# Pair interactions of a recommendation tower: products summed in groups of eight, larger rings, and fills placed between doubles

## The chip, the cores and the metric

The kernel runs on one core of a Trainium2 chip. The metric is the device time of one execution in microseconds, the median over several executions.

## The reference

For each of 2048 samples, 32 embedding rows of 64 numbers are gathered from 32 tables. `z` holds the sum of each row (32 values). For each of the 496 pairs i < j, `outer = x_i^T K_p x_j` with a 64 x 64 kernel of the pair's own. Then a small network follows, all in fp32:

```
z     = sum(x, axis=-1)                       # 32 values
outer = einsum('bpd,pde,bpe->bp', x_i, K, x_j)  # 496 values
h = concat([z, outer, dense_ctx])             # 544 values
h = relu(h @ W1 + b1)                         # 512
h = relu(h @ W2 + b2)                         # 256
y = h @ W3                                    # 1
```

## The kernel before, in words

The batch is worked off in four quarters of 512 samples (`NQ`, `QB`). A **stage** is a pair of features: 8 indirect DMAs from GpSimd (L176), each of 128 rows of one table, fill a slot of `gathered` (ring of `GR` = 4 stages, at most 4 gathers in flight). VectorE sums the rows (L287, `sum_x`), TensorE transposes the stage into `tr` (L328), and ScalarE copies it to `x_t` (L213, `keep_x`). There are 16 stages to a quarter, and `x_t` holds two quarters.

A **double** is a step of the pair work (`DOUBLES`, 128 to a quarter). TensorE multiplies two stages' halves with kernels of `k_sb` on 64 rows of the array each, side by side (L386 and L387, `multiply`), into one of `MR` = 3 slots of `m_ps`; each fp32 matmul shows as two passes. VectorE multiplies the result with `x_t` (L300, `product`) into `prod`, a ring of `PR` = 7. A slot of `m_ps` is free when its product is done: double p waits for product p - 3. TensorE then sums the products over partitions with 0/1 columns of `sel` into the bank `acc` (L398, `reduce`), for two doubles (a **quad**) with four matmuls side by side, and a product waits until the quad that read its slot of `prod` has been reduced. Doubles come in groups of `GROUP` = 4, and after the doubles of group g the two quads of group g - 1 are reduced. After 8 groups ScalarE copies `acc` to a block of `z_sb` (L247, `keep_z`); there are 4 blocks and a short one with the sums and `dense_ctx`.

All of `tr`'s users stand in one written order. `BEFORE` and `AFTER` give, by quarter and group, the **fills** ahead of a group's doubles or behind its reduction: transposed stages ("x"), the z sums ("s", L335), and the three layers of the quarter before ("h1" L339 and L341, "h2" L347, "y" L353). TensorE, ScalarE and VectorE walk the same order. In the first quarter stages are transposed close to their first use; stage a of a later quarter is transposed behind group 18 + 2a counted from the start of the quarter before, and its gathers are issued from three groups earlier on, each waiting for one more product (L170). The gathers of a stage also wait until the stage four places back is transposed and summed. The last quarter's layers run at the end (`layer1` into `m_ps`), after the last `keep_z`.

SyncE's queue loads indices, kernels (`k_sb`) and weights at the start, then per quarter the dense context and the store of `y`.

Of the kernel before, what the change touches and what calls it, by code (L numbers as in the profile page):

```python
# [6 lines left out]
DENSE, H1, H2 = 16, 512, 256  # L7
P = 128
NQ = 4
# [4 lines left out]
GR = 4  # L14
IN_FLIGHT = 4
PR = 7
# [19 lines left out]
GROUP = 4  # L36
# [3 lines left out]

GROUPS_OF_BLOCK = 8
NB = NG // GROUPS_OF_BLOCK
SUM_ROWS = F
ZLAST = SUM_ROWS + DENSE


def row_of(quad):
    return quad // (2 * GROUPS_OF_BLOCK), quad % (2 * GROUPS_OF_BLOCK)  # L50

# [4 lines left out]

BEFORE, AFTER = {}, {}


def group_of_stage(q, a):

    return 18 + 32 * (q - 1) + 2 * a


for _a in range(STAGES):
    _g = 0 if _a < 3 else min(FIRST[_a] // GROUP - (_a > 5), (4 * _a - 7) // 3)
    BEFORE.setdefault((0, _g), []).append(("x", 0, _a))
for _q in range(1, NQ):  # L70
    for _n in range(H1 // P):
        AFTER.setdefault((_q, 1 + 2 * _n), []).append(("h1", _q - 1, _n))
    for _n in range(H2 // P):
        AFTER.setdefault((_q, 9 + 2 * _n), []).append(("h2", _q - 1, _n))
    AFTER.setdefault((_q, 13), []).append(("y", _q - 1, 0))
    for _a in range(STAGES):
        AFTER.setdefault(divmod(group_of_stage(_q, _a), NG), []).append(("x", _q, _a))
    AFTER.setdefault((_q, 18), []).append(("s", _q, 0))
AFTER.setdefault((0, NG - 1), []).append(("s", 0, 0))
ORDER = [e for q in range(NQ) for g in range(NG) for e in BEFORE.get((q, g), []) + AFTER.get((q, g), [])]  # L80
PLACE = {e: n for n, e in enumerate(ORDER)}

def dlrm_tower(nc, ids, tables, kmat, dense_t, w1, b1, w2, b2, w3, out):
# [6 lines left out]
    with ctx:  # L90
# [13 lines left out]
        z_sb = sb("z_sb", [P, NB + 1, QB])  # L104
        z_nat = sb("z_nat", [P, 2, TILES, SUM_ROWS])
        w1_sb = sb("w1_sb", [P, NB + 1, H1])
# [48 lines left out]
        def _(pool):  # L155
# [5 lines left out]
            for G in range(NQ * STAGES):  # L161
# [4 lines left out]
                for n in range(GATHERS):  # L166
                    t, f = divmod(n, 2)
                    if q:

                        pool.wait_ge(prod_ready, GROUP * (group_of_stage(q, a) - 3) + n)  # L170
                    k = G * GATHERS + n
                    if k >= IN_FLIGHT:
# [4 lines left out]
                        out=gathered[:, G % GR, t, f, :], out_offset=None, in_=tables[2 * (STAGES - 1 - a) + f],  # L177
# [4 lines left out]
        def _(sp):  # L182
# [10 lines left out]
            for q in range(NQ):  # L193

                if q:
                    sp.wait_ge(tr_kept, place("h1", q - 1, H1 // P - 1))
                sp.dma_start(z_sb[SUM_ROWS:ZLAST, NB, :], dense_t[:, q * QB:(q + 1) * QB]).then_inc(dense_loaded, 16)
# [8 lines left out]
        def _(act):  # L206
            def keep_x(q, a):
                act.wait_ge(tr_filled, place("x", q, a))
                if q >= 2 and a == 0:

                    act.wait_ge(prod_ready, (q - 1) * ND)
                    act.wait_ge(reduced, (q - 1) * QUADS)
                nc.scalar.activation(x_t[:, q % 2, a, :], tr[:], ACT.Copy).then_inc(tr_kept, 1)  # L213
# [15 lines left out]
            def keep_sums(q):  # L229
                act.wait_ge(tr_filled, place("s", q, 0))  # L230
                nc.scalar.activation(z_sb[0:SUM_ROWS, NB, :], tr[0:SUM_ROWS, :], ACT.Copy).then_inc(tr_kept, 1)
# [13 lines left out]
            def keep_z(q, b):  # L245
                act.wait_ge(reduced, q * QUADS + 2 * GROUPS_OF_BLOCK * (b + 1))
# [3 lines left out]
            for q in range(NQ):  # L250
                for g in range(NG):
                    for what in BEFORE.get((q, g), ()):
                        keep(*what)
                    if g and g % GROUPS_OF_BLOCK == 0:
                        keep_z(q, g // GROUPS_OF_BLOCK - 1)
                    if g == 0 and q:
                        keep_z(q - 1, NB - 1)
                    for what in AFTER.get((q, g), ()):
                        keep(*what)
# [218 lines left out]
```

## Time and profile before

| what | us |
|---|---|
| median of 3 runs | 1012.58 (1011.55 to 1014.28) |
| the profiled execution | 1018.13 |
| its span in the profile | 1016.3 |
| TensorE busy, share of the span | 886.5, 87% |
| VectorE busy | 641.3, 63% |
| GpSimd busy | 483.6, 48% |
| ScalarE busy | 69.3, 7% |
| mean granted TensorE clock | 0.963 |
| product on VectorE, one | 1.219 (x512) |
| one gather on GpSimd | 0.943 (x512) |

Busy time of TensorE counts matmuls with modelled ends, so 87% is not 87% of its peak. The product's groups of instructions show 302.5 us of idle VectorE ahead of them, ended mostly by TensorE's matmuls of L387. The 40 slices of the span show TensorE at 9 tenths only from slice 9 on; ahead of that it is at 0 to 8 tenths and the granted clock falls to 5 tenths in places.

### The profile page before, as it was taken

How to read it: one execution, taken by the hardware profiler on the slowest of the kernel's cores; microseconds unless marked ns; L12 is line 12 of the kernel's file. 1: busy time of each engine (PE TensorE's matmuls, PEld its weight loads, DVE VectorE, ACT ScalarE, POOL GpSimd, SP SyncE). 2: the span in 40 equal slices, each digit the busy share in tenths (PEclk: the TensorE clock that was granted, in tenths of full speed). 3: DMA queues.
4: the chain of work that ended last, by engine and by line, in shares of the span. 5: the costliest groups of instructions: out<-in, count | busy, mean ns of one | idle time of the engine just before them, and what ended most of it. 6: DMA issues, size and time to landing. Idle time of an engine off the chain costs nothing.

```text
span 1016.3 us, 11896 instructions
## 1 busy us (share of the span) xinstructions
PE 886.5 (87%) x4608; PEld 311.6 (31%) x4608; DVE 641.3 (63%) x579; ACT 69.3 (7%) x113; POOL 483.6 (48%) x518
## 2 busy tenths in 40 slices
PE   0323579699999999998999999998999999999998
PEld 0111123223333333333333333323333333333333
DVE  0102257578887575687877656676787657688850
ACT  0000000000000001000000101000000101000001
POOL 5774735536565444555666444554556445400000
PEclk9956779999999999999999999999999999999999
DMA  9310101101111000110111010011101000000000
GB/s 348 107 27 15 27 14 19 21 12 23 23 21 23 17 17 18 20 21 20 22 23 22 15 19 17 19 22 19 21 19 24 15 17 19 19 1 1 1 1 0
DMA packets 19777, 28.20 MB, mean 28 GB/s; under 512 B 8901, under 2 KB 9413, under 8 KB 18825
## 3 DMA queue, kind: packets, MB, share of 16 engines
q0 software_dynamic: 16384, 16.81, 8.6%
q1 hardware_dynamic: 3336, 10.63, 2.9%
q8 instruction: 37, 0.61, 0.3%
q14 instruction: 20, 0.16, 0.1%
HBM read 27.40 MB, written 0.01 MB: 27 GB/s over the span
## 4 chain that ended last, share of the span: by engine, by line
PE 77%; another core or an unknown queue 8%; issue 7%; DVE 4%; DMA 2%; ACT 1%; SPq 1%; POOL 1%; DVEq 0%; POOLq 0%
PE m_ps L386 39%; PE acc L398 21%; PE tr L341 4%; DVE prod L300 3%; PE tr L328 3%; PE tr L347 2%; PE m_ps L387 2%; DMA w_sb<-in_w 2%; PE m_ps L341 1%; PE tr L339 1%; PE m_ps L347 1%; PE tr L353 1%; POOL gathered L176 1%; SPq L186 1%
## 5 line engine op out<-in xcount | busy, mean ns | idle before, releaser
L300 DVE TENSOR_TENSOR prod<-m_ps,x_t 128x1024 f32<-128x1024 f32 x512 | 604.3, 1219 | 302.5 <-PE m_ps L387 180.7
L176 POOL DMA_INDIRECT gathered<-in_tbl,idx x512 | 482.9, 943 | 403.4 <-DVE prod L300 178.2
L386 PE MATMUL m_ps<-x_t,k_sb 64*128 64x512 f32 x1024 | 501.4, 623 | 74.6 <-DVE prod L300 35.6
L387 PE MATMUL m_ps<-x_t,k_sb 64*128 64x512 f32 x1024 | 502.3, 624 | 0.0
L386 PEld LDWEIGHTS m_ps<-x_t,k_sb 64*128 64x128 f32 x1024 | 180.7, 191 | 346.9 <-issue 261.6
L398 PE MATMUL acc<-prod,sel 128*32 128x512 f32 x2048 | 247.0, 600 | 0.0
L387 PEld LDWEIGHTS m_ps<-x_t,k_sb 64*128 64x128 f32 x1024 | 180.6, 191 | 0.0
L398 PEld LDWEIGHTS acc<-prod,sel 128*32 128x32 f32 x2048 | 53.7, 109 | 176.5 <-issue 119.6
L328 PE MATMUL tr<-ident,gathered 128*128 128x128 f32 x256 | 44.5, 299 | 50.6 <-DMA gathered<-in_tbl,idx 41.4
L213 ACT ACTIVATE x_t<-tr 128x512 f32<-128x512 f32 x64 | 38.2, 597 | 471.7 <-PE tr L328 275.3
L287 DVE TENSOR_REDUCE z_nat<-gathered 128x8 f32<-128x512 f32 x64 | 43.1, 675 | 38.1 <-DMA gathered<-in_tbl,idx 38.1
L328 PEld LDWEIGHTS tr<-ident,gathered 128*128 128x128 f32 x256 | 28.5, 147 | 100.7 <-issue 87.4
L341 PE MATMUL tr<-z_sb,w_sb 128*128 128x512 f32 x96 | 44.4, 605 | 0.0
L341 PEld LDWEIGHTS tr<-z_sb,w_sb 128*128 128x128 f32 x96 | 17.2, 189 | 26.3 <-issue 26.3
L247 ACT ACTIVATE z_sb<-acc 128x512 f32<-128x512 f32 x16 | 9.6, 597 | 202.4 <-PE acc L398 129.5
L347 PE MATMUL tr<-h_sb,w_sb 128*128 128x512 f32 x48 | 22.2, 605 | 0.0
L217 ACT ACTIVATE h_sb<-tr,b_sb 128x512 f32<-128x512 f32 x12 | 8.2, 687 | 112.3 <-PE tr L341 112.3
L341 PE MATMUL m_ps<-z_sb,w_sb 128*128 128x512 f32 x32 | 14.8, 605 | 0.0
L339 PE MATMUL tr<-z_sb,w_sb 48*128 48x512 f32 x24 | 13.5, 641 | 0.0
L347 PEld LDWEIGHTS tr<-h_sb,w_sb 128*128 128x128 f32 x48 | 8.6, 189 | 13.6 <-issue 13.6
L341 PEld LDWEIGHTS m_ps<-z_sb,w_sb 128*128 128x128 f32 x32 | 5.8, 189 | 8.8 <-issue 8.8
L353 PE MATMUL tr<-h_sb,w_sb 128*1 128x512 f32 x16 | 7.5, 592 | 0.8 <-ACT h_sb L268 0.8
(24 smaller groups left out, 39.6 us busy)
## 6 DMA issues: line engine op xcount, KB each, us to landing
gathered<-in_tbl,idx POOLq DMA_INDIRECT x512
k_sb<-in_kmat SPq DMA_DIRECT2D x7, 1024.0 KB, 14.3
w_sb<-in_w SPq DMA_DIRECT2D x1, 1280.0 KB
k_sb<-in_kmat SPq DMA_DIRECT2D x2, 256.0 KB, 4.2
k_sb<-in_kmat SPq DMA_DIRECT2D x1, 512.0 KB, 6.4
w_sb<-in_w SPq DMA_DIRECT2D x1, 512.0 KB
idx<-in_ids SPq DMA_DIRECT2D x1, 256.0 KB, 2.7
z_sb<-in_dense_t SPq DMA_DIRECT2D x4, 32.0 KB
```

Of the source, the lines that this page charges most:

```text
L176: nc.gpsimd.indirect_dma_start(out=gathered[:, G % GR, t, f, :], out_offset=None, in_=tables[2 * (STAGES - 1 - a) + f], in_offset=bass.Ind ...
L213: nc.scalar.activation(x_t[:, q % 2, a, :], tr[:], ACT.Copy).then_inc(tr_kept, 1)
L287: nc.vector.tensor_reduce(z_nat[:, q % 2, :, 2 * a:2 * a + 2], gathered[:, G % GR, :, :, :], axis=AX.X, op=ALU.add).then_inc(x_summed, 1)
L300: nc.vector.tensor_tensor(prod[:, p % PR, :, :], m_ps[:, p % MR, :, :], other, ALU.mult).then_inc(prod_ready, 1)
L328: last = nc.tensor.transpose(tr[:, t * P:(t + 1) * P], gathered[:, G % GR, t, :, :].rearrange("p f d -> p (f d)"), ident[:])
L339: nc.tensor.matmul(to, w1_sb[0:ZLAST, NB, n * P:(n + 1) * P], z_sb[0:ZLAST, NB, :], start=True, stop=False)
L341: last = nc.tensor.matmul(to, w1_sb[:, b, n * P:(n + 1) * P], z_sb[:, b, :], start=False, stop=(b == NB - 1))
L347: last = nc.tensor.matmul(to, w2_sb[:, c, n * P:(n + 1) * P], h1_sb[:, c, :], start=(c == 0), stop=(c == H1 // P - 1))
L353: last = nc.tensor.matmul(to, w3_sb[:, c:c + 1], h2_sb[:, c, :], start=(c == 0), stop=(c == H2 // P - 1))
L386: nc.tensor.matmul(m_ps[:, p % MR, 0, :], k_sb[0:D, d, :], x_t[0:D, q % 2, a0, :], start=True, stop=True)
L387: nc.tensor.matmul(m_ps[:, p % MR, 1, :], k_sb[D:P, d, :], x_t[D:P, q % 2, a1, :], start=True, stop=True).then_inc(unit_done, 1)
L398: last = nc.tensor.matmul(acc[c * 32:c * 32 + 32, :], sel[:, 30 - 2 * row:62 - 2 * row], prod[:, (q * ND + 2 * n + c // 2) % PR, c % 2, :] ...
```

## The change

- `GROUP` is 8 and a quarter has 16 groups. A group's four quads are reduced in one go after the fifth double of the next group (`BEHIND` = 5). A block of `z_sb` is 4 such groups.
- `PR` is 12. `x_t` is one ring of `XR` = 20 stages in place of two quarters; `keep_x` waits until the last product that uses the old stage is done.
- `BEFORE`/`AFTER` become `AHEAD`, by single doubles: a fill stands ahead of a double. In the first quarter stage a comes three doubles ahead of its use, the last five earlier. In later quarters stage a comes at double 88 + 8a from the start of the quarter before, "h1" ahead of doubles 11, 19, 27, 35, "h2" 43 and 51, "y" 59, the z sums 84. Gathers are issued from 24 doubles ahead of their transpose.
- Layer one at the end is cut in two: short block and blocks 0 and 1 for all four outputs ahead of the wait for the last `keep_z`, blocks 2 and 3 behind it.
- `gathered` has the tiles outermost; `DENSE` has another spelling.

```diff
-PR = 7
+XR = 20
+PR = 12
-GROUP = 4
+GROUP = 8
+BEHIND = 5
...
+LAST_USE = [0] * STAGES
+for _d, _e in enumerate(DOUBLES):
+    for _a in _e:
+        LAST_USE[_a] = _d
-GROUPS_OF_BLOCK = 8
+GROUPS_OF_BLOCK = 4
...
-def group_of_stage(q, a):
-    return 18 + 32 * (q - 1) + 2 * a
+def step_of_stage(q, a):
+    return ND * (q - 1) + 88 + 8 * a
...
-    _g = 0 if _a < 3 else min(FIRST[_a] // GROUP - (_a > 5), (4 * _a - 7) // 3)
-    BEFORE.setdefault((0, _g), []).append(("x", 0, _a))
+    _s = FIRST[_a] - 3
+    AHEAD.setdefault((0, max(0, min(_s, 86 - 2 * (STAGES - 1 - _a))) if _a > 1 else 0), []).append(("x", 0, _a))
...
-        x_t = sb("x_t", [P, 2, STAGES, QB])
-        gathered = sb("gathered", [P, GR, TILES, 2, D])
+        x_t = sb("x_t", [P, XR, QB])
+        gathered = sb("gathered", [P, TILES, GR, 2 * D])
...
-                        pool.wait_ge(prod_ready, GROUP * (group_of_stage(q, a) - 3) + n)
+                        pool.wait_ge(prod_ready, step_of_stage(q, a) - 24 + n)
...
             for q in range(NQ):
-                for g in range(NG):
-                    for what in BEFORE.get((q, g), ()):
+                for d in range(ND):
+                    for what in AHEAD.get((q, d), ()):
                         fill(*what)
-                    for d in range(GROUP * g, GROUP * (g + 1)):
-                        multiply(q, d)
-                    if g:
-                        reduce(q, g - 1)
-                    elif q:
-                        reduce(q - 1, NG - 1)
-                    for what in AFTER.get((q, g), ()):
-                        fill(*what)
+                    multiply(q, d)
+                    if d % GROUP == BEHIND - 1:
+                        if d >= GROUP:
+                            reduce(q, d // GROUP - 1)
+                        elif q:
+                            reduce(q - 1, NG - 1)
             reduce(LAST, NG - 1)
             pe.wait_ge(dense_loaded, 16 * NQ)
+            pe.wait_ge(tr_kept, place("s", LAST, 0))
+            pe.wait_ge(z_kept, NQ * NB - 1)
+            pe.wait_ge(prod_ready, NQ * ND)
+            for n in range(H1 // P):
+                layer1_begin(n, m_ps[:, n // 2, n % 2, :])
             pe.wait_ge(z_kept, NQ * NB)
             for n in range(H1 // P):
-                layer1(n, m_ps[:, n // 2, n % 2, :], h1_summed)
+                layer1_end(n, m_ps[:, n // 2, n % 2, :], h1_summed)
```

## Rows read from the trace of the kernel before

**Rows 1.** The page: busy us (share of the span) and instructions of an engine.
```profile
PE 886.5 (87%) x4608; PEld 311.6 (31%) x4608; DVE 641.3 (63%) x579; ACT 69.3 (7%) x113; POOL 483.6 (48%) x518
```
**Rows 2.** Windows: stretch, length, busy us of each engine, granted clock, DMA share, GB/s.
```profile
41.70:146.58 104.88, 49.81 (x197) 17.77 (x196) 31.19 (x29) 3.58 (x6) 61.70 (x66) 0.69 0.11 21
146.58:320.20 173.62, 158.84 (x900) 54.24 (x896) 131.83 (x120) 10.49 (x18) 98.34 (x105) 0.98 0.11 21
320.20:544.85 224.65, 216.83 (x1154) 76.03 (x1152) 159.56 (x145) 17.71 (x29) 120.20 (x129) 1.00 0.10 20
544.85:772.50 227.65, 218.67 (x1156) 76.69 (x1152) 159.84 (x145) 16.87 (x28) 120.64 (x129) 0.99 0.10 19
772.50:980.30 207.80, 207.78 (x1112) 73.66 (x1108) 154.29 (x137) 12.86 (x21) 57.38 (x61) 1.00 0.06 11
```
**Rows 3.** Timeline of TensorE, gathers over: start us, us, line, operation, [idle before <-releaser].
```profile
947.40 1.93 PE L398 MATMUL acc<-prod,sel 128*32 128x512 f32 x16
949.25 0.69 PE L386 MATMUL m_ps<-x_t,k_sb 64*128 64x512 f32 x1
...
949.79 0.59 PE L386 MATMUL m_ps<-x_t,k_sb 64*128 64x512 f32 x1
...
952.36 0.59 PE L386 MATMUL m_ps<-x_t,k_sb 64*128 64x512 f32 x1
...
952.89 1.06 PE L398 MATMUL acc<-prod,sel 128*32 128x512 f32 x8
```
**Rows 4.** Timeline of ScalarE: copies of transposed stages, among gathers and after them.
```profile
303.01 0.60 ACT L213 ACTIVATE x_t<-tr 128x512 f32<-128x512 f32 x1 [11.53 <-PE tr L328]
315.20 0.60 ACT L213 ACTIVATE x_t<-tr 128x512 f32<-128x512 f32 x1 [11.60 <-PE tr L328]
...
887.86 0.60 ACT L213 ACTIVATE x_t<-tr 128x512 f32<-128x512 f32 x1 [5.49 <-PE tr L328]
...
899.42 0.60 ACT L213 ACTIVATE x_t<-tr 128x512 f32<-128x512 f32 x1
```
**Rows 5.** Timeline of VectorE, among gathers and after them.
```profile
290.57 0.68 DVE L287 TENSOR_REDUCE z_nat<-gathered 128x8 f32<-128x512 f32 x1
291.16 4.85 DVE L300 TENSOR_TENSOR prod<-m_ps,x_t 128x1024 f32<-128x1024 f32 x4
...
309.30 1.23 DVE L300 TENSOR_TENSOR prod<-m_ps,x_t 128x1024 f32<-128x1024 f32 x1 [1.18 <-PE m_ps L387]
...
950.43 3.49 DVE L300 TENSOR_TENSOR prod<-m_ps,x_t 128x1024 f32<-128x1024 f32 x3 [0.60 <-PE m_ps L387]
```
**Rows 6.** Timeline of TensorE among gathers, around that product.
```profile
308.08 0.59 PE L386 MATMUL m_ps<-x_t,k_sb 64*128 64x512 f32 x1
...
310.67 0.66 PE L386 MATMUL m_ps<-x_t,k_sb 64*128 64x512 f32 x1 [0.28 <-DVE prod L300]
```
**Rows 7.** Timeline of GpSimd and TensorE in the first quarter.
```profile
187.66 0.95 POOL L176 DMA_INDIRECT gathered<-in_tbl,idx  x1 [2.21 <-issue]
...
216.84 0.94 POOL L176 DMA_INDIRECT gathered<-in_tbl,idx  x1 [10.77 <-DVE z_nat L287]
...
203.90 1.19 PE L386 MATMUL m_ps<-x_t,k_sb 64*128 64x512 f32 x1 [6.45 <-issue]
```
**Rows 8.** Chain that ended last, in order of time: start us, us, what.
```profile
349.48 1.05 PE tr L339 x2
350.53 3.63 PE tr L341 x8
...
366.78 3.63 PE tr L341 x8
```
**Rows 9.** Waits of TensorE from 320.2 to 980: us in total, times, longest.
```profile
PE tr L328 <- ACT z_sb L231: 4.5, 2, 2.4
```
**Rows 10.** Timeline of TensorE at the end of the pair work.
```profile
984.78 1.09 PE L339 MATMUL m_ps<-z_sb,w_sb 48*128 48x512 f32 x2 [0.81 <-ACT z_sb L247]
```
**Rows 11.** Windows: the stretch behind the longest of those waits.
```profile
687.00:692.30 5.30, 4.10 (x14) 2.12 (x16) 1.00 (x1) 1.18 (x2) 0.68 (x1) 0.68 0.04 6
```

More of the change, by code:

```diff
@@ L76 @@
     for _a in range(STAGES):
[L77 to L80, printed above, removed]
+        AHEAD.setdefault(divmod(step_of_stage(_q, _a), ND), []).append(("x", _q, _a))
+    AHEAD.setdefault((_q, 84), []).append(("s", _q, 0))
+ORDER = [e for q in range(NQ) for s in range(ND) for e in AHEAD.get((q, s), [])]
@@ L81 @@
 PLACE = {e: n for n, e in enumerate(ORDER)}
+KEEP_Z = {GROUP * GROUPS_OF_BLOCK * b + BEHIND - 1: b - 1 for b in range(1, NB)}
+KEEP_LAST_Z = BEHIND - 1
 def dlrm_tower(nc, ids, tables, kmat, dense_t, w1, b1, w2, b2, w3, out):
@@ L208, in keep_x @@
                 act.wait_ge(tr_filled, place("x", q, a))
[L209 to L213, printed above, removed]
+                G = q * STAGES + a
+                if G >= XR:
+                    old_q, old_a = divmod(G - XR, STAGES)
+                    act.wait_ge(prod_ready, old_q * ND + LAST_USE[old_a] + 1)
+                nc.scalar.activation(x_t[:, G % XR, :], tr[:], ACT.Copy).then_inc(tr_kept, 1)
             def keep_h1(q, n):
@@ L250, in _ @@
             for q in range(NQ):
-                for g in range(NG):
-                    for what in BEFORE.get((q, g), ()):
+                for s in range(ND):
+                    for what in AHEAD.get((q, s), ()):
                         keep(*what)
-                    if g and g % GROUPS_OF_BLOCK == 0:
-                        keep_z(q, g // GROUPS_OF_BLOCK - 1)
-                    if g == 0 and q:
+                    if s in KEEP_Z:
+                        keep_z(q, KEEP_Z[s])
+                    if q and s == KEEP_LAST_Z:
                         keep_z(q - 1, NB - 1)
-                    for what in AFTER.get((q, g), ()):
-                        keep(*what)
             keep_z(LAST, NB - 1)
@@ L336, in sums, with layer1_begin, layer1_end @@
                 last.then_inc(tr_filled, 1)
-            def layer1(n, to, done):
-                nc.tensor.matmul(to, w1_sb[0:ZLAST, NB, n * P:(n + 1) * P], z_sb[0:ZLAST, NB, :], start=True, stop=False)
-                for b in range(NB):
+            def layer1_begin(n, to):
+                nc.tensor.matmul(to, w1_sb[0:ZLAST, ZSHORT, n * P:(n + 1) * P], z_sb[0:ZLAST, ZSHORT, :],
+                                 start=True, stop=False)
+                for b in range(NB - 2):
+                    nc.tensor.matmul(to, w1_sb[:, b, n * P:(n + 1) * P], z_sb[:, b, :], start=False, stop=False)
+            def layer1_end(n, to, done):
+                for b in (NB - 2, NB - 1):
                     last = nc.tensor.matmul(to, w1_sb[:, b, n * P:(n + 1) * P], z_sb[:, b, :],
@@ L385, in multiply @@
                     pe.wait_ge(prod_ready, p - MR + 1)
-                nc.tensor.matmul(m_ps[:, p % MR, 0, :], k_sb[0:D, d, :], x_t[0:D, q % 2, a0, :], start=True, stop=True)
-                nc.tensor.matmul(m_ps[:, p % MR, 1, :], k_sb[D:P, d, :], x_t[D:P, q % 2, a1, :],
+                nc.tensor.matmul(m_ps[:, p % MR, 0, :], k_sb[0:D, d, :], x_t[0:D, (q * STAGES + a0) % XR, :],
+                                 start=True, stop=True)
+                nc.tensor.matmul(m_ps[:, p % MR, 1, :], k_sb[D:P, d, :], x_t[D:P, (q * STAGES + a1) % XR, :],
                                  start=True, stop=True).then_inc(unit_done, 1)
@@ L393, in reduce @@
                     pe.wait_ge(z_kept, q * NB + g // GROUPS_OF_BLOCK)
-                for n in (2 * g, 2 * g + 1):
+                for n in range(GROUP // 2 * g, GROUP // 2 * (g + 1)):
                     _, row = row_of(n)
@@ L449 @@
                     continue
-                p = pair_index(min(i, j), max(i, j))
-                k_l[half * D:half * D + D, d, t * D:t * D + D] = k_in[p] if i < j else k_in[p].T
-                w1_l[b, 32 * ((d % 2) * 2 + half) + 2 * row + t] = w1_in[F + p]
+                k_l[half * D:half * D + D, d, t * D:t * D + D], w1_l[b, 32 * ((d % 2) * 2 + half) + 2 * row + t] = pair(i, j)
     for f in range(F):
-        w1_l[NB, F - 2 - 2 * (f // 2) + f % 2] = w1_in[f]
-    w1_l[NB, SUM_ROWS:ZLAST] = w1_in[w1_in.shape[0] - DENSE:]
+        w1_l[ZSHORT, F - 2 - 2 * (f // 2) + f % 2] = w1_in[f]
+    w1_l[ZSHORT, SUM_ROWS:ZLAST] = w1_in[w1_in.shape[0] - DENDE:]
     arrays = {
```

66 lines of the change are left out of this document (34 added, 32 removed).

## The prediction

> **What bounds the kernel now.** I read the busy shares first, then the stretches, then single instructions of each. TensorE is busy for 87% of the span [rows 1], but matmul ends are modelled, so the share says only where to look. By stretches [rows 2] the span falls into four parts: doubles 0 to 23 (104.9 us, TensorE busy for 49.8 and at a mean granted clock of 0.69), doubles 24 to 127 (173.6), quarters one and two (224.7 and 227.7), quarter three up to its last two reductions (207.8). The last part has almost no gathers and is TensorE at its pace: from one reduction to the next 952.89 - 947.40 = 5.49 us [rows 3], which is 12 passes (8 of the four doubles, 4 of the reduction, 0.429 each from 949.79 and 952.36) or 5.14, and 0.35 of switching.
>
> The stages with gathers are slower. With gathers over, two groups with one transposed stage take 899.42 - 887.86 = 11.56; with gathers on, 315.20 - 303.01 = 12.19 [rows 4]. A difference of 0.6 per eight doubles is not TensorE's work. The row that shows it is the first product after a reduction: in the tail its double's second pass begins 0.64 ahead of it (949.79, 950.43) [rows 3, 5], among gathers 1.22 ahead (308.08, 309.30) [rows 5, 6], and the fourth double of the group then waits until 310.67. VectorE's product chain is therefore just critical after each reduction, twice per eight doubles. The worst such delays come in long unbroken runs of gathers: 15 gathers from 187.66 with no pause (the next is at 216.84, after 10.77 idle), and in it TensorE stands for 6.45 us before 203.90 [rows 7]. I call such late completions slips; what makes them the trace does not say.
>
> **Part 1: eight doubles per reduction.** Removed: one of two switches per eight doubles, 0.35. Added: a reduction of 8 passes in one go, in which only three filled slots of m_ps stand ready for VectorE (MR stays 3; 12 product slots do not help, since a double needs an m_ps slot). Step by step, from t, the start of the second pass of the double ahead of a reduction:
> - reduction begins at t + 0.53 (952.36 to 952.89), takes 1.85 for four passes (947.40 to 949.25), so 1.85 + 4 x 0.43 = 3.57 for eight; the next double's second pass is 0.54 later: t + 4.64 [rows 3];
> - its product starts 0.64 later: t + 5.28. VectorE has long run dry, its three products took only 3.4;
> - the next double that a reduction follows needs the fifth product from here (slot free). Products follow each other by (3.48 - 1.22)/2 = 1.13 [rows 5]: the fifth starts at t + 9.80 and ends at t + 11.02;
> - TensorE's waiting double then has its second pass 0.65 after that end (309.30 + 1.23 = 310.53; the double starts at 310.67, a second pass follows 0.5 later, as 949.25 and 949.79) [rows 3, 5, 6]: t' = t + 11.67.
> TensorE alone would need 2 x 5.49 - 0.35 = 10.63. So the cycle without a transposed stage goes from 10.98 to **11.67**, bound by the chain of five products. With a stage, the sum over the gathered rows (0.59 of VectorE, 290.57 to 291.16 [rows 5]) lies in that chain: **12.26**, against 11.56 without and 12.19 with slips.
>
> **Part 2: fills between doubles.** Layer-one fills stand before double 11, 19, ...: in the middle of the chain, and give VectorE 4.3 us to catch up. There TensorE bounds both. One such period is 366.78 - 350.53 = 16.25 [rows 8]; less 0.35, plus 0.15 because transposes no longer share the reduction's switch: **16.05**. Four of these, two of layer two (without the 1.05 of the short block, 15.0 [rows 8]) and one of layer three (10.63 + 0.58 + 0.15 for TensorE's cycle with a stage, and 4 passes: 13.1) make 107.3 for seven cycles. Moving the z sums from beside a stage's transposes (group 18) to double 84 removes two waits of TensorE for ScalarE's copy, 4.5 us in all [rows 9]; it leaves 0.7 per quarter of its own.
>
> **Part 3: quarters one and two.** Each: 9 x 12.26 + 107.3 + 0.7 = 218.3. Slips to be added: only one window per cycle, the product after the reduction, is still exposed, the others now have about 1 us of slack (double 9's matmul is done about 1.0 before its product can start), and the gathers pause there, since they wait for products too. Bounds: 0 and 0.6 per cycle (the delay above); I take 0.3, the middle, since the row of 0.6 is from a window with gathers in front: 18 x 0.3 = 5.4. 436.6 + 5.4 = 442.0 against 452.3: **-10.3** (-15.7 to -4.9).
>
> **Part 4: quarter three to the last reduction.** Stages stand up to double 80: 4 x 12.26 + 107.3 + 0.7 + 4 x 11.67 = 203.7 to double 504; then 4.9 to the double before a reduction (the cycle less its reduction and three doubles), the four quads (4.1), three doubles (2.6) and the last four quads (3.5): 15.2 in sum. 218.9 against 211.5 (to 984.0, the 0.81 ahead of 984.78 [rows 10]): **+7.4**. This is the surest term, no gather is near.
>
> **Part 5: the first quarter.** Doubles 0 to 23: stages 3 to 5 are transposed three doubles ahead of their use instead of right before; that hides a round trip to ScalarE but makes TensorE stand for the gather with fewer doubles behind it. Bounds -20 and +12 (a fifth and a ninth of a stretch that is half waiting); I take 0. Doubles 24 to 127: stages 11 to 15 move from doubles 48, 52, 60, 64, 68 to 57, 69, 81, 84, 86. The ring of four then lets gathers run in eights with pauses, and the run of [rows 7] goes. Now the stretch loses (173.6 - 13 x 11.56 - 6.5)/13 = 1.3 per cycle outside that run; with one window of two left I take 0.8. Up to double 81, 7.1 cycles of 12.26 + 0.8 = 93. From 81 on stages 1 to 7 of the next quarter are gathered in one run, since the ring frees late (13 us behind their pacing, gaining 2 us a stage). The trace has no run there; below by 0, above by 25 (half of a 50 us run, nearest to [rows 7]); the run ends itself as doubles slow down, so I take 7: 72 + 7 = 79. Sum 172.0 against 173.6, and two quads fewer reduced by double 128 (-1.7, repaid in part 4): **-3.3** (-23 to +25 with both unknowns).
>
> **Part 6: the end.** Begun sums of layer one fill the wait for the last copy, ahead of the matmul at 984.78 [rows 10], 0.81, and its switch: **-0.9**; nothing else in the tail moves.
>
> **At nothing:** the ring of 20 stages (stage 4 waits for product 113 when double 120 is due, seven doubles earlier; if it were late, each double of delay is 1.4), the new gathered layout (same shapes; the sum's 0.68 [rows 5] is hidden only outside the chain, so a change of it by 0.1 costs 2.5 over 25 stages), the twelve products, fewer waits on PE. SP's queue is not passed by anything moved; ScalarE is idle beside its copies.
>
> **Sum:** -10.3 + 7.4 - 3.3 - 0.9 = -7.1 on an execution of 1018.13 (span 1016.3). That execution is 5.5 above the median of 1012.58; taken off the median: **1005.5 us**.
>
> **The Trainium skill, weighed.** The late products stand beside gathers that GpSimd issues. The Trainium skill, "SBUF — State Buffer", section "SBUF: two separate sides", says that on the engine side only GpSimd and VectorE contend, by a lock, and TensorE and ScalarE wait on nobody. Here TensorE's own completions come late [rows 7], so that rule would have gathers cost nothing: part 3 would be -15.7 and part 5 lose its 7, for 993. I stay with the rows.
>
> **Rivals.**
> - *The startup waits go.* If the slips of doubles 0 to 81 shrink with shorter gather runs, a fifth of 104.9 comes back: 1005.5 - 20 = 985. For: half of that stretch is waiting [rows 2]. Against: stages 0 to 7 are gathered in one run in both.
> - *The product chain pays every slip.* If quarters one and two keep what they lose now (452.3 less 2 x 213.3 at TensorE's pace, that is 9 x 11.56 + 108.7 (107.3 and 0.2 for each of seven) + 0.6 each, and less 4.5: 21, or 1.2 per cycle), part 3 becomes +5.5: 1021, slower. It decides once the mean cycle with a stage and no fill is over 12.95 (12.56 + 7.1/18). For: the cycle has no slack left. Against: one window instead of two.
> - *The long run of gathers after double 81.* As in [rows 7], TensorE stands for half of a 50 us run: 25 instead of 7, so 1023, slower. It decides from some 14 us lost between doubles 81 and 127.
> - *The clock falls.* After the wait of 2.4 at the z sums the granted clock was 0.68 over 5.3 us [rows 11], between 1.2 and 2.4 GHz: 1.7 lost. If the new waits of up to 1 us in each of some 27 cycles did the same, 46 would be added: 1050. Against: beside today's waits of 0.5 per cycle the clock is 1.00 [rows 2]. The Trainium skill, "TensorE: Matmul & The Clock Gate", section "A second HAM failure mode: psum-queue depth-cycling", tells of such a loss from short waits between groups; the trace does not agree so far.
>
> **Chances.** Forecast 0.50 (994 to 1014; 0.39 faster, 0.08 same, 0.03 slower), startup 0.20 (all faster), chain 0.15 (0.03 same, 0.12 slower), long run 0.12 (0.01 same, 0.11 slower), clock 0.03. That is 0.59 faster by over 0.3%, 0.12 within 0.3%, about what a measurement can tell from no change, and 0.29 slower. The range 984 to 1022 leaves out the clock, and the ends of the startup and long-run cases.
>
> **What would show it.** Right: tail reductions 11.6 to 11.7 apart with TensorE waiting for products before the fourth and fifth double after each; layer-one cycles near 16.05; the last layer's first matmul right behind the last reduction. Wrong: tail cycles at 10.6 (then the chain was not binding), stage cycles over 12.95, or double 128 reached after 330.

## The result, and the profile after

| | median us | runs | profiled execution, its span |
|---|---|---|---|
| before | 1013.43 | 1011.55 to 1015.83 (4) | 1018.13, 1016.3 |
| after | 1024.72 | 1023.78 to 1026.49 (4) | 1023.78, 1021.9 |

The changed kernel is slower: ratio 1.0112, 95% interval 1.0085 to 1.0139, 11.3 us. The forecast was 1005.5, range 984 to 1022: wrong in sign, and the time lies outside the range. The windows of the changed kernel's profile, cut at the same doubles as [rows 2] (columns as there), with the end of the span as a row of its own:

```profile
41.67:139.00 97.33, 43.11 (x182) 15.09 (x184) 29.45 (x28) 3.46 (x6) 59.49 (x64) 0.77 0.12 22
139.00:321.75 182.75, 164.69 (x894) 55.94 (x894) 128.96 (x119) 10.07 (x18) 95.97 (x102) 0.95 0.11 19
321.75:546.20 224.45, 219.71 (x1154) 75.89 (x1154) 157.13 (x144) 17.27 (x29) 119.92 (x129) 1.00 0.11 20
546.20:771.35 225.15, 220.04 (x1154) 75.69 (x1154) 158.67 (x146) 17.20 (x29) 121.44 (x129) 1.00 0.11 20
771.35:990.30 218.95, 217.76 (x1160) 74.76 (x1160) 156.00 (x141) 14.21 (x23) 61.36 (x66) 1.00 0.06 11
990.30:1021.90 31.60, 27.85 (x64) 10.13 (x60) 0.00 (x0) 5.30 (x8) 0.00 (x0) 1.00 0.00 0
```

Against [rows 2]: double 128 is reached 1.5 later (321.75, 320.2), quarters one and two take 449.6 instead of 452.3, quarter three up to the end of its last reduction 218.95 instead of 211.5, and what follows 31.6 instead of 32.3. Spans differ by 5.6, medians by 11.3: the profiled execution of before was 4.7 above its median, that of after 0.9 below.

A **cycle** is the work of eight doubles. The cycle without gathers shows the new limit. TensorE's timeline, beside [rows 3]:

```profile
945.58 3.64 PE L416 MATMUL acc<-prod,sel 128*32 128x512 f32 x32
949.15 0.69 PE L403 MATMUL m_ps<-x_t,k_sb 64*128 64x512 f32 x1
...
949.68 0.59 PE L403 MATMUL m_ps<-x_t,k_sb 64*128 64x512 f32 x1
```

VectorE's timeline of the same stretch, beside [rows 5]:

```profile
950.33 9.29 DVE L315 TENSOR_TENSOR prod<-m_ps,x_t 128x1024 f32<-128x1024 f32 x8 [2.32 <-PE m_ps L405]
961.94 3.49 DVE L315 TENSOR_TENSOR prod<-m_ps,x_t 128x1024 f32<-128x1024 f32 x3 [2.32 <-PE m_ps L405]
```

VectorE has eight products in one unbroken run, then stands dry (without a finished double) for 2.32 us: 11.61 from run to run. TensorE's own work in that time is 10.6. The product follows its double's second pass by 0.65 (949.68, 950.33), so nothing is late here. Among gathers the first product behind a reduction is late. VectorE and TensorE of the changed kernel in quarter two:

```profile
730.77 3.49 DVE L315 TENSOR_TENSOR prod<-m_ps,x_t 128x1024 f32<-128x1024 f32 x3 [3.09 <-PE m_ps L405]
734.18 0.68 DVE L300 TENSOR_REDUCE z_nat<-gathered 128x8 f32<-128x512 f32 x1
734.77 5.89 DVE L315 TENSOR_TENSOR prod<-m_ps,x_t 128x1024 f32<-128x1024 f32 x5
743.74 3.49 DVE L315 TENSOR_TENSOR prod<-m_ps,x_t 128x1024 f32<-128x1024 f32 x3 [3.09 <-PE m_ps L405]
```
```profile
741.80 0.69 PE L403 MATMUL m_ps<-x_t,k_sb 64*128 64x512 f32 x1
...
742.33 0.59 PE L403 MATMUL m_ps<-x_t,k_sb 64*128 64x512 f32 x1
```

743.74 - 742.33 = 1.41 instead of 0.65: 0.76 late, and the dry time is longer by 0.77 (3.09, 2.32). The cycle is 12.97.

In the first quarter, a stage that waits in the run of gathers behind double 81 (TensorE; ScalarE, whose copies of the two stages ahead of it these are; GpSimd, whose 13 gathers between the two shown have pauses of 0.3):

```profile
240.26 0.66 PE L339 MATMUL tr<-ident,gathered 128*128 128x128 f32 x4
...
252.50 1.09 PE L339 MATMUL tr<-ident,gathered 128*128 128x128 f32 x4 [9.66 <-DMA gathered<-in_tbl,idx]
```
```profile
234.60 0.60 ACT L228 ACTIVATE x_t<-tr 128x512 f32<-128x512 f32 x1 [2.77 <-PE tr L339]
251.75 0.60 ACT L228 ACTIVATE x_t<-tr 128x512 f32<-128x512 f32 x1 [16.55 <-remote]
```
```profile
234.06 0.94 POOL L191 DMA_INDIRECT gathered<-in_tbl,idx  x1 [8.83 <-issue]
...
256.76 0.94 POOL L191 DMA_INDIRECT gathered<-in_tbl,idx  x1 [4.29 <-DVE prod L315]
```

The profile puts this wait down to the gathers, but the last gather of the waiting stage was issued at 224.28. What TensorE stands for is the bank `tr`: the stage transposed at 240.26 is copied only at 251.75, 11.49 later, where the copy of the stage ahead of it, outside the run, starts 0.69 behind its transpose (233.91, 234.60). The copy ends at 252.35, and TensorE goes on at 252.50. So the completion of the transpose is late, as that of the doubles is, and by much more.

At the end, the short block of layer one follows the last reduction at once, where [rows 10] has 0.81 of waiting:

```profile
986.76 3.64 PE L416 MATMUL acc<-prod,sel 128*32 128x512 f32 x32
990.34 1.12 PE L350 MATMUL m_ps<-z_sb,w_sb 48*128 48x512 f32 x2
```

### The profile page after: what moved, and what is told of

Same layout as the page of the kernel before. It is cut to its first block, busy times and chain, and to the rows that moved or that the text cites. A ratio compares the mean times of both kernels' runs of the same rounds, so it can differ in the third digit from the quotient of the medians.

```text
span 1021.9 us, 11934 instructions
## 1 busy us (share of the span) xinstructions
PE 896.6 (88%) x4608; PEld 309.9 (30%) x4608; DVE 632.5 (62%) x579; ACT 70.1 (7%) x113; POOL 483.7 (47%) x518
## 3 DMA queue, kind: packets, MB, share of 16 engines
q0 software_dynamic: 16384, 16.81, 9.2%
## 4 chain that ended last, share of the span: by engine, by line
PE 73%; DVE 3%; issue 3%; another core or an unknown queue 2%; DMA 0%; ACT 0%; DVEq 0%
PE m_ps L403 39%; PE acc L416 20%; DVE prod L315 3%; PE tr L339 2%; PE tr L353 2%; PE tr L363 2%; PE tr L357 2%; PE tr L350 1%; PE m_ps L405 1%; PE m_ps L353 1%; PE tr L369 1%; PE m_ps L363 1%; PE m_ps L357 1%; DVE z_nat L300 0%
## 5 line engine op out<-in xcount | busy, mean ns | idle before, releaser
L403 PE MATMUL m_ps<-x_t,k_sb 64*128 64x512 f32 x1024 | 523.2, 629 | 63.5 <-issue 31.7
L405 PE MATMUL m_ps<-x_t,k_sb 64*128 64x512 f32 x1024 | 524.8, 630 | 0.0
L403 PEld LDWEIGHTS m_ps<-x_t,k_sb 64*128 64x128 f32 x1024 | 171.5, 189 | 366.6 <-issue 297.7
L416 PE MATMUL acc<-prod,sel 128*32 128x512 f32 x2048 | 233.0, 595 | 0.0
L405 PEld LDWEIGHTS m_ps<-x_t,k_sb 64*128 64x128 f32 x1024 | 171.3, 189 | 0.0
L416 PEld LDWEIGHTS acc<-prod,sel 128*32 128x32 f32 x2048 | 60.0, 109 | 163.4 <-issue 139.9
```

Of the source, the lines that this page charges most:

```text
L403: nc.tensor.matmul(m_ps[:, p % MR, 0, :], k_sb[0:D, d, :], x_t[0:D, (q * STAGES + a0) % XR, :], start=True, stop=True)
L405: nc.tensor.matmul(m_ps[:, p % MR, 1, :], k_sb[D:P, d, :], x_t[D:P, (q * STAGES + a1) % XR, :], start=True, stop=True).then_inc(unit_done, 1)
L416: last = nc.tensor.matmul(acc[c * 32:c * 32 + 32, :], sel[:, 30 - 2 * row:62 - 2 * row], prod[:, (q * ND + 2 * n + c // 2) % PR, c % 2, :] ...
```

## The experiments

The kernel before ran beside every group of experiments, and it did not stand still: 1012 to 1016 at first, 1027 to 1041 beside e1 to e4 and e11 to e13, 931 to 935 beside r1, r2 and e5 to e10. The record names the same chip, number 9, for the group of e1 to e4 and for that of r1, r2, e5 and e6, so the chip alone does not set the level. Absolute times are therefore compared within a group only; ratios are to the kernel before in the same group. Medians and the stretches of the profiles, in us ("to double 128" is all that lies ahead of it from the start of the span, then quarters one and two together, then quarter three to the end of its last reduction):

| run | median | before beside it | ratio, 95% | to double 128 | one and two | three |
|---|---|---|---|---|---|---|
| before (first profile) | | | | 320.2 | 452.3 | 211.5 |
| after (first profile) | 1024.72 | 1013.43 | 1.0112 (1.0085 to 1.0139) | 321.8 | 449.6 | 219.0 |
| e1 after, no late gathers | 998.24 | 1033.87 | 0.9674 (0.9634 to 0.9715) | 308.0 | 437.3 | 218.9 |
| e2 before, no late gathers | 993.39 | 1033.87 | 0.9629 (0.9588 to 0.9670) | 317.6 | 428.1 | 210.9 |
| e3 groups of four | 1036.50 | 1033.87 | 1.0041 (1.0020 to 1.0063) | 334.4 | 453.1 | 216.7 |
| e4 last stages evenly | 1019.77 | 1033.87 | 0.9879 (0.9847 to 0.9910) | 314.6 | 451.6 | 219.9 |
| r1 after again | 947.29 | 933.39 | 1.0149 (1.0134 to 1.0164) | 258.1 | 437.3 | 218.9 |
| r2 before again | 932.83 | 933.39 | 0.9994 (0.9985 to 1.0003) | 258.2 | 428.1 | 210.9 |
| e5 gathers behind product | 946.78 | 933.39 | 1.0144 (1.0129 to 1.0160) | 256.8 | 437.3 | 218.9 |
| e6 sums behind reduction | 931.64 | 933.39 | 0.9981 (0.9972 to 0.9989) | 254.1 | 427.3 | 216.6 |
| e7 groups of four again | 922.89 | 934.37 | 0.9878 (0.9863 to 0.9893) | 248.6 | 428.0 | 212.2 |
| e8 after, half products | 913.53 | 934.37 | 0.9772 (0.9757 to 0.9787) | 245.8 | 424.0 | 211.1 |
| e9 before, half products | 933.43 | 934.37 | 0.9994 (0.9984 to 1.0003) | 258.0 | 428.1 | 210.9 |
| e10 before, small parts | 931.40 | 934.37 | 0.9966 (0.9952 to 0.9979) | 260.8 | 426.5 | 210.9 |
| e11 four, evenly | 1021.62 | 1034.92 | 0.9881 (0.9847 to 0.9916) | 319.8 | 451.7 | 216.8 |
| e12 after, third time | 1031.06 | 1034.92 | 0.9959 (0.9936 to 0.9982) | 326.7 | 452.0 | 219.3 |
| e13 last stages evenly again | 1020.94 | 1034.92 | 0.9875 (0.9842 to 0.9908) | 316.2 | 452.1 | 219.3 |

**e1 and e2: gathers of the later quarters left out.**

```diff
-            for G in range(NQ * STAGES):
+            for G in range(STAGES):
...
-                    dve.wait_ge(landed, (G + 1) * GATHERS // IN_FLIGHT * 16)
+                    dve.wait_ge(landed, (min(G, STAGES - 1) + 1) * GATHERS // IN_FLIGHT * 16)
...
```


> The changed kernel with the gathers of quarters one to three left out (those quarters work on the first quarter's last four stages, so that part of the result is not computed). The first quarter up to double 81 is as in the changed kernel. My theory: a cycle of eight doubles with a transposed stage is 13.0 us in the changed kernel because the chain of five products needs 12.2 and gathers make the first product after a reduction 0.8 late; without gathers it falls to 12.2 to 12.3, quarters one and two together from 449.6 to about 437, quarter three stays within 1.5 of 218.9. Rival (the lateness comes with the long reduction or with the transposed stage, not with gathers): the cycle stays at 13.0 and quarters one and two at 449. Doubles 81 to 127 lose the stand behind the long run of gathers too, some 10 us. In all 1024.7 falls to about 1002; by the rival to 1014.

> The kernel before with the gathers of quarters one to three left out in the same way. My theory: its cycle with a stage falls from 12.2 to 13 to TensorE's 11.56, quarters one and two together from 452.3 to 427 to 431 (two waits of 2 for the z sums stay), quarter three stays at 211. In all 1013.4 falls to about 990. If gathers are what makes products late, then without them the kernel before is faster than the changed one by more than with them (12 to 20 instead of 11), since only the chain of products is left to tell them apart. Rival: the cycle stays over 12 and the time over 1005.

ScalarE's copies of stages in quarter two, first of e1, then of e2:

```profile
708.59 0.60 ACT L228 ACTIVATE x_t<-tr 128x512 f32<-128x512 f32 x1 [2.73 <-PE tr L339]
720.79 0.60 ACT L228 ACTIVATE x_t<-tr 128x512 f32<-128x512 f32 x1 [11.61 <-PE tr L339]
```
```profile
716.97 0.60 ACT L213 ACTIVATE x_t<-tr 128x512 f32<-128x512 f32 x1 [10.96 <-PE tr L328]
728.53 0.60 ACT L213 ACTIVATE x_t<-tr 128x512 f32<-128x512 f32 x1 [10.96 <-PE tr L328]
```

The cycle is 12.20 and 11.56, and quarters one and two take 437.3 and 428.1. Beside them, in the same group, e3 and e4 with their gathers have cycles of 13.1. The lateness needs the gathers; the rival, that it comes with the long reduction or the transposed stage, falls. The expected times of these two were near (998 for 1002, 993 for 990), though the kernel before stood 20 higher; the difference between the two was 4.9, less than the 12 to 20 that I had put, since e1's first quarter was 9.6 shorter than e2's.

**r1 and r2: the two kernels once more.**

> The changed kernel once more, unchanged, beside the kernel before on one chip. The kernel before took 1013.4 beside the changed one's 1024.7, and 1033.9 beside the experiments so far, so the two have to be taken side by side. If the verdict of the first comparison holds, the changed kernel is 1.1% above the kernel before here too. If the kernel before is the one that varies by chip (its products are late twice per cycle, the changed kernel's once), the changed kernel stands near 1024 and is 0 to 1.2% faster.

> The kernel before once more, to see in a profile which stage makes up the 20 us between its two medians. My theory: the first quarter and the cycles with gathers (first quarter 320.3 in the first profile, quarters one and two 452.3), with quarter three's cycles without gathers at 10.98 as before. Rival: every stage is slower alike (a chip with a lower clock), with the tail cycle above 10.98.

Here the same programs, gathers and all, run without late products. VectorE of r1 in quarter two, and ScalarE of r2:

```profile
656.44 3.49 DVE L315 TENSOR_TENSOR prod<-m_ps,x_t 128x1024 f32<-128x1024 f32 x3 [2.32 <-PE m_ps L405]
659.84 0.68 DVE L300 TENSOR_REDUCE z_nat<-gathered 128x8 f32<-128x512 f32 x1
660.43 5.89 DVE L315 TENSOR_TENSOR prod<-m_ps,x_t 128x1024 f32<-128x1024 f32 x5
668.64 3.49 DVE L315 TENSOR_TENSOR prod<-m_ps,x_t 128x1024 f32<-128x1024 f32 x3 [2.32 <-PE m_ps L405]
```
```profile
657.72 0.60 ACT L213 ACTIVATE x_t<-tr 128x512 f32<-128x512 f32 x1 [10.97 <-PE tr L328]
669.28 0.60 ACT L213 ACTIVATE x_t<-tr 128x512 f32<-128x512 f32 x1 [10.96 <-PE tr L328]
```

Their windows from double 24 on, r1 first:

```profile
97.30:258.05 160.75, 158.62 (x896) 54.42 (x895) 128.82 (x119) 10.09 (x18) 113.47 (x121) 1.00 0.13 25
258.05:476.55 218.50, 216.52 (x1154) 77.14 (x1155) 157.63 (x145) 17.23 (x29) 120.56 (x128) 1.00 0.10 20
476.55:695.35 218.80, 216.59 (x1154) 77.20 (x1156) 157.91 (x146) 17.25 (x29) 120.69 (x129) 1.00 0.10 20
695.35:914.20 218.85, 217.70 (x1161) 75.18 (x1162) 156.14 (x141) 14.27 (x24) 61.43 (x66) 1.00 0.05 11
914.20:945.60 31.40, 27.66 (x60) 9.98 (x60) 0.00 (x0) 5.29 (x8) 0.00 (x0) 1.00 0.00 0
```
```profile
99.50:258.15 158.65, 153.94 (x902) 55.38 (x898) 132.41 (x120) 10.66 (x18) 116.50 (x124) 0.99 0.14 26
258.15:472.15 214.00, 213.23 (x1153) 77.15 (x1152) 159.68 (x144) 17.66 (x29) 120.10 (x129) 1.00 0.10 21
472.15:686.25 214.10, 213.33 (x1158) 77.20 (x1154) 160.31 (x145) 17.07 (x28) 120.52 (x129) 1.00 0.10 21
686.25:897.10 210.85, 210.85 (x1144) 74.75 (x1140) 156.66 (x138) 12.93 (x21) 57.40 (x61) 1.00 0.06 11
897.10:929.50 32.40, 27.84 (x64) 10.14 (x60) 0.00 (x0) 5.30 (x8) 0.00 (x0) 1.00 0.00 0
```

This is the change where products are on time: -0.1 to double 128, +9.2 in quarters one and two, +8.0 in quarter three, -1.0 at the end: 16.1 of span, ratio 1.0149. Both kernels lose by lateness: before 62 us to double 128 and 24 in quarters one and two, after 64 and 12 (first profiles against these). In quarter three the cycles without gathers are 10.98 and 11.61 in both groups, so the rival to r2, every stage slower alike, falls. Part of the loss ahead of double 128 is the clock, which falls where TensorE stands: from double 81 to 128 of the changed kernel (231.1 to 321.75) the granted clock was 0.92, where r1 has 1.00 (183.7 to 258.05), and right behind the stand of 9.66 us above a pass of a double took 1.22 instead of 0.69.

**e8 and e9: half of each product.** These two leave out the other half of every product; the reductions read the one half twice.

```diff
...
-                nc.vector.tensor_tensor(prod[:, p % PR, :, :], m_ps[:, p % MR, :, :], other, ALU.mult).then_inc(prod_ready, 1)
+                nc.vector.tensor_tensor(prod[:, p % PR, 0, :], m_ps[:, p % MR, 0, :], other, ALU.mult).then_inc(prod_ready, 1)
...
-                                                prod[:, (q * ND + 2 * n + c // 2) % PR, c % 2, :],
+                                                prod[:, (q * ND + 2 * n + c // 2) % PR, 0, :],
```


> The changed kernel with VectorE's product on one half of a double only, 512 columns instead of 1024 (the other half's products are not computed; the reductions read the one half twice). My theory: at 0.6 us per product the chain of five no longer binds, TensorE does: the cycle without a stage falls from 11.61 to 10.6, with a stage from 12.26 to 11.4, and cycles with layer one stay at 16.1. Rival (it is the long reduction itself, by its place in TensorE's queue, that costs): the cycles stay at 11.6 and 12.3.

> The kernel before with the product halved in the same way. My theory: it is already bound by TensorE, so the cycle without a stage stays at 10.98 and with a stage at 11.56, and where products come on time the time falls by less than 5; beside it the changed kernel with half products is 5 to 12 faster, which is what the removed switches are worth once VectorE is out of the way. Rival: both fall alike and the changed kernel stays slower.

TensorE's reductions in the tail of e8:

```profile
849.44 3.64 PE L413 MATMUL acc<-prod,sel 128*32 128x512 f32 x32
860.08 3.64 PE L413 MATMUL acc<-prod,sel 128*32 128x512 f32 x32
```

10.64, TensorE's own pace, for the same order of instructions: VectorE's chain of five products sets the 11.61, not the long reduction in TensorE's queue. The kernel before does not move (ratio 0.9994). With VectorE out of the way the changed kernel (e8) is 20 us faster than the kernel before treated alike (e9), more than my 5 to 12: 12 of it lie ahead of double 128, which I had not counted.

**e3 and e7: groups of four in the changed kernel.**

```diff
-GROUP = 8
-BEHIND = 5
+GROUP = 4
+BEHIND = 4
...
-GROUPS_OF_BLOCK = 4
+GROUPS_OF_BLOCK = 8
```


> The changed kernel with groups of four again (two quads reduced behind every fourth double), everything else as changed: rings of 12 and 20, fills between doubles, last layer begun early. My theory: the chain after a reduction is then one product long, so cycles without a stage go from 11.61 back to 10.98 and quarter three from 218.9 to about 212; cycles with a stage to 11.7 plus late products, 12.3 to 12.8; in all 5 to 12 below the changed kernel, 1013 to 1020. Rival (the fills between doubles or the larger rings cost, not the groups): quarter three stays at 218 and the time at 1024.

> The changed kernel with groups of four again, a second time, since the comparison of the first time had products delayed for both kernels (the kernel before at 1034). My theory: the chain behind a reduction is one product long, so the tail cycle is 10.98, a cycle with a stage 11.6 without late products, quarters one and two 424 to 428 and quarter three 210 to 211, where the kernel before has 428.1 and 210.9: where products are on time it is 3 to 6 below the kernel before and 17 to 20 below the changed one. Rival (the fills between doubles cost as much as the groups): it stays within 3 of the changed kernel, 10 or more above the kernel before.

e3 was a miss: quarter three 216.7 for 212, cycles with a stage 13.1 for 12.3 to 12.8, and slower than the kernel before. With products on time (e7) it is near what the theory says (quarter three 212.2 for 210 to 211), reductions at 5.49 again and copies of stages 11.56 apart:

```profile
863.05 1.92 PE L416 MATMUL acc<-prod,sel 128*32 128x512 f32 x16
868.54 1.93 PE L416 MATMUL acc<-prod,sel 128*32 128x512 f32 x16
```
```profile
618.69 0.60 ACT L228 ACTIVATE x_t<-tr 128x512 f32<-128x512 f32 x1 [5.49 <-PE tr L339]
630.25 0.60 ACT L228 ACTIVATE x_t<-tr 128x512 f32<-128x512 f32 x1 [10.97 <-PE tr L339]
```

922.89 is 24.4 below the changed kernel of the neighbouring group (their kernels before differ by 1.0) and 1.2% below the kernel before; my 3 to 6 below was too little, again for the first quarter (248.6, 258.2). So where products are on time the groups of eight cost about 2.6%, and the rest of the change gains 1.2%. Where products are late that does not hold: e3 stands at 1.0041 and the changed kernel (e12) at 0.9959, each of the kernel before beside it. Groups of four have two first products per cycle to be late, groups of eight one, and the cycle with a stage and gathers is 13.1 in e3 and 13.0 in the changed kernel: the lateness takes back what the shorter chain gives.

**e6: the row sums behind the reduction.**

```diff
-    AHEAD.setdefault((_q, 84), []).append(("s", _q, 0))
+    AHEAD.setdefault((_q, 92), []).append(("s", _q, 0))
...
-                        if what == "x":
+                        if what == "x" and not h:
                             sum_x(h, a)
+                    if d % GROUP == BEHIND:
+                        for what, h, a in AHEAD.get((q, d - BEHIND), ()):
+                            if what == "x" and h:
+                                sum_x(h, a)
```


> The changed kernel with VectorE's sums over the rows of a stage of later quarters moved from ahead of double 0 of eight to ahead of double 5, where VectorE has run dry behind a reduction (the z sums move from double 84 to 92 for that). My theory: the sum leaves the chain of five products, so the cycle with a stage falls by 0.59, from 13.0 to 12.4 among gathers and from 12.2 to 11.6 without; about 25 cycles, 12 to 16 below the changed kernel; cycles with layer one do not move. Rival (TensorE and its transposes set the cycle, the chain does not): no difference.

15.7 below the changed kernel, at the upper end of the 12 to 16 that were put: 10.0 in quarters one and two, 4.0 ahead of double 128 and 2.3 in quarter three. The sum of a stage was put at 0.59 per cycle, and the cycle fell from 12.20 to 11.61. VectorE runs eight products in a row, and the sum stands in its dry time, 655.83 - 644.22 = 11.61:

```profile
644.22 9.29 DVE L315 TENSOR_TENSOR prod<-m_ps,x_t 128x1024 f32<-128x1024 f32 x8 [1.73 <-PE m_ps L409]
653.43 0.68 DVE L300 TENSOR_REDUCE z_nat<-gathered 128x8 f32<-128x512 f32 x1
655.83 6.88 DVE L315 TENSOR_TENSOR prod<-m_ps,x_t 128x1024 f32<-128x1024 f32 x6 [1.73 <-PE m_ps L409]
```

**e4, e13, e12 and e11: the last stages of the first quarter.**

```diff
-    _s = FIRST[_a] - 3
-    AHEAD.setdefault((0, max(0, min(_s, 86 - 2 * (STAGES - 1 - _a))) if _a > 1 else 0), []).append(("x", 0, _a))
+    _s = max(0, FIRST[_a] - 3 if _a < 12 else 57 + 15 * (_a - 11) // 2)
+    AHEAD.setdefault((0, _s), []).append(("x", 0, _a))
```


> The changed kernel with the last four stages of the first quarter transposed ahead of doubles 64, 72, 79 and 87 instead of 69, 81, 84 and 86. My theory: the ring of four then comes free evenly, the run of 15 gathers at 234 to 253 and the stand of 9.7 us for a stage in it go, and doubles 80 to 95 take about 26 instead of 39.4: 10 to 14 below the changed kernel, 1011 to 1015. Rival (the first quarter's waits only move, since the gathers are what bounds it): double 128 is reached at 321 as before and the time stays at 1024.

> The changed kernel with the evenly spaced last stages again, beside the unchanged one. My theory: 1 to 3 below the changed kernel where products are on time (only the waits of doubles 80 to 87 go), 7 to 14 below where they are late in long runs of gathers, since it was at 1019.8 with double 128 at 315. Rival: no difference in either.

> The changed kernel once more, unchanged. My theory: 1.1 to 1.5% above the kernel before wherever the two stand side by side, 947 beside 933 where products are on time. Rival (the loss comes from one place only): within 0.3% in this comparison.

> The changed kernel with groups of four and the last four stages of the first quarter ahead of doubles 64, 72, 79 and 87. My theory: groups of four give 1.2% below the kernel before where products are on time (922.9 beside 934.4); the even spacing removes most of the 2 us above the pace in doubles 80 to 87, so 0 to 3 below groups of four alone, 920 to 923 beside 934. Where gathers make products late, the first quarter gains 10 or more from the spacing and groups of four alone gain nothing (1036.5 beside 1033.9), so 1.0% to 1.5% below the kernel before. Rival (the spacing has no effect of its own): as groups of four alone, 1.2% below and none.

e4 had no changed kernel beside it, so it was run again as e13. e13 is 10.1 below e12 beside it, and all of it lies ahead of double 128 (316.2, 326.7). TensorE's transposes of e12, then of e4, around double 81:

```profile
243.89 0.66 PE L339 MATMUL tr<-ident,gathered 128*128 128x128 f32 x4
259.75 1.09 PE L339 MATMUL tr<-ident,gathered 128*128 128x128 f32 x4 [13.28 <-ACT x_t L228]
```
```profile
231.97 0.66 PE L339 MATMUL tr<-ident,gathered 128*128 128x128 f32 x4
245.56 0.66 PE L339 MATMUL tr<-ident,gathered 128*128 128x128 f32 x4
```

Stages close together in the order free the ring of four late and then all at once, and TensorE stands for 13.28. The expectation for e12 missed: where the kernel before is at 1035, the changed one is 0.4% faster, not 1.1% slower. The sign of the whole change depends on how late products are. e11 is the version to keep: 1.2% below the kernel before with late products; e7, the same but for the spacing, is 1.2% below with products on time. What makes the 1.2% of e11 is the spacing: with groups of eight it gives the same (e13, 0.9875), and without it groups of four are at 1.0041 (e3). What the even spacing adds where products are on time was not run, with groups of four or of eight.

**e10 and e5.**

```diff
-    AFTER.setdefault((_q, 18), []).append(("s", _q, 0))
+    AFTER.setdefault((_q, 19), []).append(("s", _q, 0))
...
```


> The kernel before with two small parts of the change alone: the last layer one begun on complete blocks ahead of the last copy, and the z sums one group away from a stage's transposes (behind group 19 instead of 18). My theory: 0.9 from the end, and TensorE's wait for the copy of the z sums, 1.3 in each of two quarters where products are on time and over 2 where they are late: 3 to 6 below the kernel before in all. Rival: nothing, since the wait for the copy is replaced by another of the same length.

(e10 also has the last layer one begun early, as in the change.) The median is 3.0 below. Against r2's profile, e10's has 0.8 less in each of quarters one and two and 0.9 less at the end, but 2.6 more ahead of double 128, so that the two spans are alike (929.6, 929.5); the profiles bear out 2.5 of the 3.0 by place, and the small size of it is not settled.

```diff
-                        pool.wait_ge(prod_ready, step_of_stage(q, a) - 24 + n)
+                        pool.wait_ge(prod_ready, step_of_stage(q, a) - 26)
```


> The changed kernel with the eight gathers of a stage in the later quarters all waiting for one product, the first behind a reduction (double 5 of eight), instead of one more product each. The run of eight takes 10.0 us, so it ends about a microsecond ahead of the end of the next reduction. If gathers just issued make TensorE's completion late, the first product behind a reduction is on time again (0.64 after its second pass instead of 1.41) and the cycle with a stage goes from 13.0 to 12.3 to 12.5: 8 to 13 below the changed kernel. If it is the length of an unbroken run that counts (8 instead of 6), the cycle stays or grows to 13.5: 0 to 10 above.

Inconclusive: in its group products were on time in every kernel, so it had nothing to cure.

## Why the prediction was wrong, step by step

- **Part 1, the chain of five products: right.** 11.67 put, 11.61 measured (11.61 in r1); 12.26 with a stage put, 12.20 measured wherever products are on time. e8 shows the mechanism by taking VectorE out of the way, e6 by taking the sum out of the chain. Where products are on time this alone makes the change slower, +9.2 and +8.0 us in r1 against r2. The prediction had these numbers (436.6 against 2 x 213.3, and +7.4) and set them off against 21 us that late products and 4.5 that the z sums cost the kernel before there, of which the changed one was to keep 5.4.
- **Part 2: right.** Cycles with layer one measured 16.11 for 16.05, with layer two 15.26 for 15.0, with layer three 13.43 for 13.1. e10 shows that moving the z sums is worth 0.8 in a quarter with products on time; with late ones [rows 9] has waits of over 2, and what moving them is worth there was not run.
- **Part 3 is the step that failed.** Without slips it gave 436.6, and 437.3 was measured (e1, r1). The slips were put at 0.3 per cycle, because "the gathers pause there". They don't: the last of six gathers in a run is issued at 741.37, just ahead of the double at 741.80. The slips measured 449.6 - 437.3 = 12.3, or 0.68 for each of the 18 cycles with a stage: 6.9 more than the 5.4 that were put. With the 0.7 above that is the whole way from -10.3 to the measured -2.7. "One window of two" was right: lateness costs the kernel before 24 us in quarters one and two and the changed one 12. But that saving of 12 is there only where products are late; with products on time these quarters are 9.2 slower.
- **Part 4: right**, +7.4 put and measured.
- **Part 5: failed by 4.8** (-3.3 put, +1.5 measured). Doubles 0 to 23 gained 7.6 (97.3 for 104.9), where I took 0; doubles 24 to 127 took 182.8 for 172.0. Up to double 81 the sum held (92.4 for 93); from there it was 90.4 for 79. Without the run of gathers I had 72, and r1 has 74.3, so the run cost 16 to 18 us where 7 was taken (bound 25). e13 and e12 size its cure at 10.
- **Part 6: right**, 0.7 to 1.0 for 0.9.
- **The base.** Parts 3 and 5 leave 12.4 of the way from -7.1 to the measured +5.6 of span. The medians lie 5.7 further apart than the spans. A sum made against one profiled execution was taken off the median: that execution had 4.7 more than its median, and nothing in the sum asked which stage held it; the profiled execution of after had 0.9 less than its own.

Of the rivals, the long run of gathers (1023) came nearest, and by its own condition: it was to decide from some 14 us lost behind double 81, and 18 were. It was given 0.12. The product chain (1021, given 0.15) fell just short of its condition, a mean cycle with a stage of 12.89 for 12.95. That two parts came out slower than forecast and the first 24 doubles faster makes the nearness of 1023 to 1024.7 partly luck. All these chances were argued from one profile, as if lateness were a property of the kernel. It is not: r2 is the same program 80 us faster. The weighed rule of the Trainium skill ("SBUF — State Buffer", section "SBUF: two separate sides", by which TensorE waits on nobody) would have gathers cost nothing; r1 agrees with it and the first profiles do not, with e1 and e2 against e3 and e4 showing that gathers are needed for the loss. The rule is on the memory ports, though, and what is late here is a completion, so that it need not be the rule that is wrong. The clock rival fell: the granted clock is 1.00 in quarters one to three of the changed kernel, new waits and all. The other rule of the Trainium skill ("TensorE: Matmul & The Clock Gate", section "A second HAM failure mode: psum-queue depth-cycling") tells of a loss from short waits between groups of matmuls that no run here shows.

**Left open:** what makes TensorE's completions late. It needs gathers, it grows with unbroken runs of them, and whole groups of runs are free of it; the gather pace on GpSimd is the same in both (0.94 us each, pauses of 0.30). e5 was meant for it and met no lateness. One more thing tells the two kinds of runs apart, in every profile of a kernel with all its gathers: with products on time the trace holds 8154 to 8189 increments of the semaphores that gathers raise when they land, with late products 3285 to 3871, for the same 16384 packets. The page of the profile gives 2.4 us from issue to landing for a gather in the first kind and no figure in the second. So the late runs differ in how semaphore increments arrive or are recorded, those of the gathers too; which of the two, and why, no run shows.

## What to carry to other kernels

A longer batch on the producer saves its switches, but the number of free slots between producer and consumer stays. Here, with three slots, a batch of 3.6 us in which nothing new is produced drains VectorE, and the chain "products until the slot is free" sets the cycle (11.61) although both engines are below it (TensorE 10.6, VectorE 9.3). Write down that chain from the end of the batch before enlarging it, and keep side work of the consumer (here 0.59 of row sums) out of it, in the time in which it is dry.

Keep transfers that share a ring evenly spaced in the order of work; stages bunched together cost 10 us here, with late products. And before taking a profile's stalls as gains to be had, run the kernel more than once, in different groups of runs: waits that differ between runs of one program are not explained by the program alone.

## What the runs showed of the hardware that was not expected

One and the same program, the kernel before, took 931 to 935, 1012 to 1016 and 1027 to 1041 us in different groups of runs. The difference is all in stretches in which GpSimd issues gathers: to double 128 it took 258.2 or 320.2, quarters one and two 428.1 or 452.3, the cycles without gathers the same (10.98 us). In the late ones the completion of a matmul is seen by others 0.6 to 0.8 us late in short runs of gathers ([rows 5, 6]; after, 743.74) and 5 us and more in runs of 15 (after, 251.75), while the matmuls behind it start at their usual pace and the ends of ScalarE's copies are still seen at once (252.35, 252.50).
